# Long attentions: ScalarE sends the maximum rows, GpSimd splits the maxima, the first batch's stacks are fetched once one chunk is stored

## The reference

```python
def _L2_xattn_ref(memory, query, seq_mask, b):        # stage 7, 8 heads of 16
    Q = _split_heads(query, H) * depth ** (-0.5)
    k_mem, v_mem = jnp.split(memory, 2, axis=2)
    logits = jnp.einsum('bhqd,bhkd->bhqk', Q, K) + b[0]
    logits = logits + -1e+30 * (1.0 - mask)
    return jnp.einsum('bhqk,bhkd->bhqd', jax.nn.softmax(logits, axis=-1), V)   # heads merged

def _L3_xattn_ref(x, context, w_qkv, w_proj, b_proj): # stage 10, 16 heads of 8
    q, k, v = split of x @ w_qkv.T
    k, v = concatenate([extra_k, k]), concatenate([extra_v, v])                # 1601 + 256 keys
    attn = softmax(jnp.einsum('bhnd,bhmd->bhnm', q * scale, k))
    return jnp.einsum('bhnm,bhmd->bhnd', attn, v) merged @ w_proj.T + b_proj
```

## Time and profile before

| What | Value |
|---|---|
| median of three runs | 4947.77 us |
| the profiled execution's own time | 4972.34 us |
| its span, first to last instruction | 4970.5 us |
| busy shares PE, DVE, ACT, POOL | 82%, 71%, 51%, 28% |
| L2544, exponentials | 688, 1024 ns each |
| L2562, reductions of a pair of banks | 576, 981 ns each |
| L2469 score products, L2488 value products | 2752, 5504 |

### The profile page before, as it was taken

One profiled execution on the slowest core, in us unless ns is written; L12 is line 12 of the kernel. 1 busy time (PEld: TensorE's weight loads), 2 busy tenths in 40 slices (PEclk: granted clock), 3 DMA queues, 4 the chain that ended last, 5 costly groups with the idle time before them and its releaser, 6 DMA issues. The chain is left out here.

```text
span 4970.5 us, 77611 instructions
## 1 busy us (share of the span) xinstructions
PE 4080.7 (82%) x29258; PEld 2235.3 (45%) x29323; DVE 3509.2 (71%) x5453; ACT 2512.4 (51%) x3544; POOL 1406.8 (28%) x1033
## 2 busy tenths in 40 slices
PE   5659796999999999999968986848995768888883
PEld 3645334666666666666643333423443332222231
DVE  5569444999997777777774455757764658888868
ACT  2133242666666666666641233535662436766772
POOL 0000300677776666666657011000000100000000
PEclk5579897999999999999978997978995779999996
DMA  0024001111110000000013016326540433223300
GB/s 19 1 109 165 27 0 57 41 47 47 34 41 1 14 1 14 14 1 1 1 55 138 0 34 138 48 46 87 78 60 4 105 71 59 46 41 54 49 2 9
DMA packets 144611, 218.53 MB, mean 44 GB/s; under 512 B 20442, under 2 KB 109036, under 8 KB 143556
## 3 DMA queue, kind: packets, MB, share of 16 engines
q1 hardware_dynamic: 136548, 197.22, 17.4%
q0 software_dynamic: 6528, 16.42, 1.4%
q10 hardware_dynamic: 1184, 0.12, 0.0%
HBM read 154.00 MB, written 56.69 MB: 42 GB/s over the span
## 5 line engine op out<-in xcount | busy, mean ns | idle before, releaser
L3114 POOL TENSOR_TENSOR arena<-arena 128x512 f32<-128x512 f32 (+1 forms) x768 | 1159.2, 1511 | 562.5 <-ACT arena L3070 503.2
L2544 ACT ACTIVATE arena<-ps 128x1024 f32<-128x1024 f32 (+1 forms) x688 | 703.9, 1024 | 335.3 <-PE ps L2469 324.8
L2562 DVE TENSOR_REDUCE arena<-ps 128x2 f32<-128x826 f32 (+1 forms) x576 | 565.0, 981 | 189.1 <-PE ps L2415 181.3
L3130 DVE TENSOR_TENSOR arena<-arena 128x1024 f32<-128x1024 f32 (+1 forms) x448 | 678.3, 1553 | 9.8 <-ACT arena L3097 9.8
L3152 DVE TENSOR_TENSOR arena<-ps,arena 128x512 f32<-128x512 f32 (+1 forms) x768 | 529.6, 690 | 121.1 <-ACT arena L3064 86.9
L2415 PE MATMUL ps<-arena 48*128 48x413 bf16 (+3 forms) x1920 | 435.1, 333 | 131.2 <-DVE arena L2562 65.4
L3064 ACT ACTIVATE arena<-ps 128x1024 f32<-128x1024 f32 (+1 forms) x448 | 412.6, 961 | 210.1 <-PE ps L2991 204.8
L2972 PE MATMUL ps<-arena 128*128 128x256 f32 (+1 forms) x1664 | 443.2, 394 | 45.5 <-DVE arena L3138 40.2
L3070 ACT ACTIVATE arena<-arena 128x1024 f32<-128x1024 f32 (+1 forms) x448 | 430.1, 993 | 93.1 <-DVE arena L3130 89.7
L2991 PE MATMUL ps<-arena 64*128 64x256 f32 (+1 forms) x3328 | 430.8, 392 | 23.4 <-DVE arena L3152 11.2
L2488 PE MATMUL ps<-arena 128*9 128x256 f32 (+2 forms) x5504 | 435.4, 389 | 10.1 <-ACT arena L2532 7.2
(11 more groups left out here) (650 smaller groups left out, 5895.6 us busy)
## 6 DMA issues: line engine op xcount, KB each, us to landing
wide_keys<-arena SPq DMA_DIRECT2D x27, 800.5 KB, 3.4
arena<-wide_keys SPq DMA_DIRECT2D x27, 800.5 KB, 4.3
arena<-in_ctx_feat SPq DMA_DIRECT2D x12, 1601.0 KB, 10.6
arena<-ctx_parts SPq DMA_DIRECT2D x96, 200.1 KB
arena<-ctx_parts SPq DMA_DIRECT2D x192, 100.1 KB
arena<-in_ctx SPq DMA_DIRECT2D x16, 768.0 KB
arena<-diff_att_stack SPq DMA_DIRECT2D x60, 192.0 KB
ctx_parts<-arena SPq DMA_DIRECT2D x24, 400.2 KB, 3.5
```

The costliest lines, as they stand in the source:

```text
L2544: act.activation(self.prob[0:rows, u % 3, :], self.ps[0:rows, 2 * (u % 2):2 * (u % 2) + 2, :].rearrange("p n c -> p (n c)"), ACT.Exp).then ...
L2562: ins = dve.tensor_reduce(dst[:, :, j // 2], self.ps[:, 4:6, 0:hi - lo], AX.X, ALU.max)
L3114: pool.tensor_tensor(acc[0:rows, u % 2, :], before, sc[0:rows, u % 2, t, :], ALU.add).then_inc(added, 1)
L3130: dve.tensor_tensor(e, e, mb[0:rows, u % 2, None, :].to_broadcast([rows, n, 2 * S]), ALU.subtract).then_inc(sub_done, 1)
```

## The change

ScalarE issues the row transfers itself behind its copy; SP only fetches units. VectorE keeps the maximum (`dve_nmax`, two buffers), GpSimd makes the three parts (`pool_split`). The turn stands one step later. The first batch's stacks are fetched as soon as chunk 0 is stored; in stage 10 the second half of the first unit's tokens goes through GpSimd's queue, and TensorE's wait for the copied own values stands behind the first looks.

```diff
     def turn_step(self, g):
-        return g * self.steps - self.lead * self.steps // self.looks + 2
+        return g * self.steps - self.lead * self.steps // self.looks + 3
...
+        if first:
+            first()
         pool.memset(self.vh[:, :, :, :, self.hd:self.hd + 1], 1.0).then_inc(s["ones_ready"], 1)
...
+        take_values(0)
+        for g in range(self.groups):
+            self.pool_split(pool, link, g)
+            b = (g - 1) // self.per_batch + 1
+            if (g - 1) % self.per_batch == 0 and b < B:
+                take_values(b)
...
     def run_sp(self, sp, stacks, values):
-        self.sp_unit(sp, 1, stacks, values)
-        for g in range(self.groups):
-            self.sp_rows(sp, g)
-            w = self.unit(g) + 2
-            if g % self.lanes == 0 and w < self.units:
-                self.sp_unit(sp, w, stacks, values)
+        for w in range(1, self.units):
+            self.sp_unit(sp, w, stacks, values)
...
         act.activation(self.max_rows[0:24, :], self.ps[0:24, 7, 0:P], ACT.Copy).then_inc(s["rows_ready"], 1)
+        act.wait_ge(s["rows_ready"], g + 1)
+        per, n = 24 // self.lanes, 4 // self.lanes
+        for e in range(self.lanes):
+            r0 = self.base(e) + self.rows
+            act.dma_start(self.qst[r0:r0 + PARTS, self.unit(g) % 4, self.slot(g, 0):self.slot(g, 0) + n, :],
+                          self.max_rows[e * per:(e + 1) * per, :]).then_inc(s["max_loaded"], 16)
...
+    def dve_nmax(self, dve, g):
+        s = self.sem
+        dve.wait_ge(s["s_free"], (g + 1) * self.looks)
+        if g >= 2:
+            dve.wait_ge(s["split_ready"], g - 1)
+        dve.tensor_reduce(self.nmax[:, g % 2, :], self.part_max[:, g % 2, :, :], AX.X, ALU.max, negate=True
+                          ).then_inc(s["nmax_ready"], 1)
+
+    def pool_split(self, pool, link, g):
+        s = self.sem
+        pool.wait_ge(s["nmax_ready"], g + 1)
         if g:
-            dve.wait_ge(s["turned_max"], g)
+            pool.wait_ge(s["turned_max"], g)
...
+        link(pool.tensor_copy(part[:, 0, :, :], nmax))
+        link(pool.tensor_tensor(left, nmax, part[:, 0, :, :], ALU.subtract))
+        link(pool.tensor_copy(part[:, 1, :, :], left))
+        pool.tensor_tensor(part[:, 2, :, :], left, part[:, 1, :, :], ALU.subtract).then_inc(s["split_ready"], 1)
...
             context(0)
-            for i in range(chunks):
...
-            sp.wait_ge(stored, chunks * PARTS * 16)
+            store(0)
+            sp.wait_ge(stored, PARTS * 16)
             queries(0)
             values(0)
+            for i in range(1, chunks):
+                store(i)
...
+                store(0)
+                store(1)
+                sp.wait_ge(first_stored, 2 * PARTS * 16)
+                tokens(sp, s["stacks_loaded"], 0, 0)
+                for i in range(2, 2 * chunks):
+                    store(i)
...
+                def first_tokens():
+                    pool.wait_ge(first_stored, 2 * PARTS * 16)
+                    tokens(pool, s["half_loaded"], 0, 1)
+                att.run_pool(pool, spans_of(full, rest, len(tiles)), first_tokens)
...
-                pe.wait_ge(own_copied, 1)
-                att.run_pe(pe)
+                att.run_pe(pe, own_copied)
```

More of the change, by code:

```diff
@@ L2297, in __init__ @@
         self.units = self.groups // lanes
+        self.half = 0
         c = -(-2 * nk // 9)
@@ L2307, in __init__ @@
         self.part_max = st.sb("part_max", [P, 2, 8, 5])
-        self.nmax = st.sb("nmax", [P, 8])
+        self.nmax = st.sb("nmax", [P, 2, 8])
         self.left = st.sb("left", [P, 8])
@@ L2338, in turn_step, with run_pool @@
     def turn_step(self, g):
-        return g * self.steps - self.lead * self.steps // self.looks + 2
-    def run_pool(self, pool, spans):
+        return g * self.steps - self.lead * self.steps // self.looks + 3
+    def run_pool(self, pool, spans, first=None):
         s = self.sem
@@ L2370, in sp_unit @@
         if w:
-            sp.wait_ge(s["stacks_loaded"], w * self.loads * 16)
+            sp.wait_ge(s["stacks_loaded"], (w * self.loads - self.half) * 16)
         if w >= 4:
@@ L2406, in pe_look @@
         if i == 0 and g % self.lanes == 0:
-            pe.wait_ge(s["stacks_loaded"], (self.unit(g) + 1) * self.loads * 16)
+            pe.wait_ge(s["stacks_loaded"], ((self.unit(g) + 1) * self.loads - self.half) * 16)
+            if g == 0 and self.half:
+                pe.wait_ge(s["half_loaded"], self.half * 16)
         if n >= 2:
@@ L2491, in pe_values, with run_pe @@
         ins.then_inc(s["pv_done"], 1)
-    def run_pe(self, pe):
+    def run_pe(self, pe, banks_free=None):
         total = self.groups * self.steps
@@ L2610, in look @@
             if n % self.looks == self.looks - 1:
-                self.dve_split(dve, link, n // self.looks)
+                self.dve_nmax(dve, n // self.looks)
         for n in range(self.looks_by(0)):
@@ L2677, in stacks @@
                 context(w)
+                if w == 4:
+                    sp.wait_ge(stored, chunks * PARTS * 16)
                 queries(w)
@@ L2684, in values, with store @@
                 sp.dma_start(att.v[0:rest, b % 2, full, :], src[full * P:SC, :]).then_inc(s["v_loaded"], 16)
-            context(0)
-            for i in range(chunks):
+            def store(i):
                 for n, ready in enumerate((high_ready, mid_ready, low_ready)):
@@ L3553, in stage10 @@
             s = att.sem
-            att.loads, att.v_loads = 6 * len(TERMS), 3
+            att.loads, att.v_loads, att.half = 6 * len(TERMS), 3, 2 * len(TERMS)
             chunks = T // BANK
@@ L3560, in stage10, with sides, tokens @@
                                     "stored", "own_ready", "own_copied"))
+            first_stored = sa.sem("first_stored")
             def place_qk(i):
                 return (i % 2) * 4 + i // 2
+            def sides(w):
+                return [(slice(64 * e, 64 * (e + 1)), lambda t, e=e: t.rearrange(
+                    "(w s e d) t -> w e d s t", w=2, e=2, d=HD3)[w % 2, e]) for e in range(2)]
+            def tokens(eng, loaded, w, e):
+                b, r = w // 2, w % 4
+                rows, side = sides(w)[e]
+                load_lane(eng, loaded, att.qst[rows, r, :, :], HD3, 0,
+                          lambda k: side(q_parts[k, :, b * S:(b + 1) * S]))
+                load_lane(eng, loaded, att.kst[rows, r, :, SC:KX], HD3, 1,
+                          lambda k: side(own_parts[k, :, b * S:(b + 1) * S]))
             block = sa.block()
@@ L3575, in context @@
                                   lambda k: side(env.ctx_parts[k, w // 2]))
[L3577 to L3583, removed]
                 def stacks(w):
                     context(w)
-                    tokens(w)
+                    if w == 4:
+                        sp.wait_ge(stored, 2 * (chunks - 1) * PARTS * 16)
+                    for e in range(2):
+                        tokens(sp, s["stacks_loaded"], w, e)
                 def values(b):
@@ L3594, in values, with store @@
                     sp.dma_start(att.v[:, b % 2, own:, :], v_own[:, b * BT:(b + 1) * BT, :]).then_inc(s["v_loaded"], 16)
-                context(0)
-                for i in range(2 * chunks):
+                def store(i):
                     for n, ready in enumerate((high_ready, mid_ready, low_ready)):
@@ L3599, in _ @@
                         sp.dma_start((q_parts, own_parts)[i % 2][n][:, i // 2 * BANK:(i // 2 + 1) * BANK],
-                                     part_qk[:, i, n, :]).then_inc(stored, 16)
-                sp.wait_ge(stored, 2 * chunks * PARTS * 16)
-                tokens(0)
+                                     part_qk[:, i, n, :]).then_inc(first_stored if i < 2 else stored, 16)
+                context(0)
+                store(0)
[4 more added lines that the diff above has]
+                    store(i)
                 sp.wait_ge(own_copied, 1)
```

30 lines of the change are left out of this document (8 added, 22 removed).

## The result

The changed kernel takes 5035.43 us (median of 4, 5030.77 to 5047.69) beside 4948.75 of the kernel before: ratio 1.0178 [1.0158, 1.0198]. Forecast was 4929. Its profiled execution took 5030.77 us, 58.4 more than that of before. That the timed runs differ by 87 us and the profiled ones by 58 is not explained; the profile of before lay 23.6 over its runs' median, that of after lies 4.7 under.

The account below looks back on a forecast made before the run. Cross-self stage: TensorE and VectorE drive each other through three look banks; memory stage: TensorE is the limit. Memory -5.5 and cross-self -13.5 make -19 us on 4947.77, so 4929; range 4888 to 4957.

Parts of the forecast that it names:

- Stall: 1.45 us: Cross-self groups: TensorE's values wait for the exponential behind ScalarE's two issues; 1.45 us in 31 groups, +45.0 us.
- the 28.8: Cross-self stage: time lost in disturbed groups, seven with rows late behind SP's values issue; all 28.8 us counted as gained.
- The turn moves one step on (+3 for +2): Cross-self group: the turn of the maxima stands one step later, TensorE reaching the dependent values at T + 1.71.
- the issue's price: ScalarE's queue: two row transfers per cross-self group take 1.47 us as on SP; 0.74 for the memory stage's one.
- ScalarE's order behind the turn: Cross-self group, T being the turn: copy T + 0.26, issues done T + 2.02, exponential done T + 3.10, values T + 3.16.
- GpSimd's split in time: GpSimd makes the split in 1.2 to 2.5 us, over 4 us before the turn, which waits for none of it.
- its saving in the cross-self stage: VectorE loses four small operations per group, 0.82 us in 31 cross-self groups: -25.4 us.
- Start: Earlier fetch after one chunk brings first looks forward: -4.5 us in the memory stage, -5 in the cross-self stage.
- Casts: Memory stage: two casts stretched to up to 1.49 us instead of 0.17 beside a GpSimd copy; -2.4 us in all.
- Rival A: Issue on ScalarE is cheap (0.45 us) or hidden: sum -37 (4911) or -64 (4884); chance 0.24.
- Rival B: ScalarE's issue is held as SP's is, seven exponentials 3 to 4 us late: +10 us (4958), slower; chance 0.16.
- Rival C: Rows still land late or the start is not earlier: -9 us, no measurable change; chance 0.12.

Follow-up runs that it names:

- the square: Four kernels: lanes_apart (SP sends, turn +2), the same at turn +3, and ScalarE sending in one piece at +2 and +3; ratios 0.9882, 0.9882, 0.9933, 1.0162.
- only_send: Kernel before the change, with ScalarE sending the rows, turn at +3 and SP only fetching units; split on VectorE, late start kept; ratio 1.0219.
- rows_on_pool: Changed kernel with the row transfers on GpSimd's queue behind its split and the turn at +1; ratio 1.0021.
- values_later: Changed kernel with SP sending the rows, turn at +2, and in the cross-self stage a batch's values issued one group later; ratio 0.9881.
- sends_apart: Changed kernel with ScalarE's two row issues behind two different exponentials and the turn at +1; ratio 1.0013.
- after_turn2: Changed kernel with only the turn put back to +2; ratio 1.0060.
- sends_apart_tied: values_later with ScalarE sending the rows in two pieces behind two exponentials, SP waiting for their landing before fetching the next unit; ratio 0.9938.
- act_busy_half: Changed kernel with SP sending the rows, turn at +3, and an idle 740-column copy on ScalarE behind each turn; ratio 1.0009.
- half_busy_later: values_later with an idle 740-column copy on ScalarE behind each turn; ratio 0.9908.
- square_act_turn2: lanes_apart with ScalarE sending the rows in one piece behind its copy, turn at +2, SP waiting for their landing; ratio 0.9933.
- lanes_apart: values_later with each cross-self unit fetched in halves, one lane behind the rows of each group; ratio 0.9882.

## Why the prediction was wrong

- **The failed step** is "Stall: 1.45 us. [...] 31 groups with a turn inside the loop: +45.0". The stall was smaller than forecast (1.25 us in the trace, 1.09 in a group's length), but its price was larger: these stops have a second price, the clock behind them. The prediction had seen that price, "the half-speed clock that follows the longer stalls is inside the 28.8", and counted it for the seven groups that lost a stall, but not for the 31 that got one. Measured: 234 us at half clock, 0.325 us each, 76 us, for the 74.6 by which the 29 groups missed; groups 0, 30 and 31 add 9.4 more. That the fitted group without the clock, 22.05, meets the forecast 22.1 is partly luck: the stall cost 1.09 for 1.45, the split saved 0.95 for 0.82, and the step of the turn, in no sum, cost 0.51. The Trainium skill, "TensorE: Matmul & The Clock Gate", section "HAM oscillation — how this bites in real kernels", tells of a loop whose waits for transfers, some 3 to 5 us each, lower the clock in every round; this trace agrees that it happens in every round, 29 groups of 29, but here no stop was over 1.52 us.
- **A second missing term**, "The turn moves one step on (+3 for +2)", was followed for ScalarE only. The step has a price of its own, 0.51 us a group, 0.23 of it at bank 7, and with it the hold throws the clock in every group. The step alone did so in none of 29 groups, the hold alone in one; that was shown only by the square.
- **Right**: the issue's price (0.73, forecast 0.74), ScalarE's order behind the turn, values at T + 3.25 (forecast T + 3.16), the late rows gone, GpSimd's split in time (1.33 us of 1.2 to 2.5), its saving in the cross-self stage (0.95 a group, forecast 0.82), the wait behind the maxima (0.16 us at 4265.30, forecast about 0.3).
- **Start**: -8.4 for -5 in the cross-self stage. The fetch began 7.4 us earlier (forecast 8.3), and the first look stood 9.1 us behind that, where 11.0 were forecast and 10.2 were before. In the memory stage -1.5 for -4.5: three stores landed 7.5 us behind the last one's issue (3335.50 to 3343.00), where the last of twelve had taken 4.2. Why is not tried.
- **Casts**: the two stretched ones are gone, and each memory group is 0.33 us shorter besides, where nothing was counted for the split. It is the split: only_send, with VectorE splitting, keeps the 22.40 us of before, and the changed kernel has 22.07.
- **Rival A**: 0.73, not 0.45. **Rival B** was the only one on the slower side and is wrong as a mechanism: ScalarE's issue took 0.73 while SP stood 4.12 in one. The sentence cited from the Trainium skill, "DMA: Bandwidth & Descriptors", section "Queues, rings and completion order", on generators that are not their own, had no such effect here: by it the hold could have reached ScalarE, and in seven issues it did not. **Rival C**'s late rows did not come true in the changed kernel (2.1 us in all); they did in later runs, whichever engine sent and whether or not SP ran ahead (rows_on_pool, values_later, sends_apart, after_turn2, sends_apart_tied).
- The slower outcome was given 0.16, 0.15 of it for rival B, a mechanism that did not occur, and no rival had the one that did.

## What to carry to other kernels

Where TensorE gets a new stop in every round of a loop, price it twice: the stop itself, and the clock, by a row of the same kernel in which a stop was followed by half clock; here two stops some 3 us apart in a group cost three times the sum of what each cost alone (4.8 us for 1.6). Put issues on a compute engine in pieces that fit its slack: 1.5 us at once cost 1.1 us a group and, with the turn a step later, 4.3; the same 1.5 in two pieces cost nothing in groups whose rows were in time. And small rows that others wait for should leave on an emptied queue: of the runs made here, those with SP as the sender were the fastest, once the values were issued one group later (0.9881 of the time before, with the split on GpSimd and the early start kept); with the units' fetch cut in two as well, every group was equal. ScalarE in two pieces was not run with that.

## What the hardware showed that was not expected

- A hold of half the length lets the clock stay up in quiet groups, but behind a disturbed one it fell again in up to four more, and once behind a quiet one (act_busy_half, half 109 us; 14 in half_busy_later). The whole hold at +2 threw it in one group of 29 with the same stop as in the others (square_act_turn2). Which stops, how close, are enough is not settled beyond the square.
- The rows landed as late as 8.6 us behind their issue beside large fetches (rows_on_pool, the group shown), and late at times whichever of SP, ScalarE and GpSimd sent them; on an emptied queue (lanes_apart) TensorE waited for none of them in groups 1 to 30.
